# Mask by activation bias, maxima turned ahead of the max rows, and reordered seams in a four-layer cross-attention kernel

## The reference, cut to what matters

```python
# x, ctx: (8 batches, 128 tokens, 128 features); 16 heads
# L0: heads of width 8, with a mask over the keys
s = einsum('bqhd,bkhd->bhqk', q, k) / sqrt(8)
s = s * m - (1 - m) * 1e10
x = layer_norm(softmax(s) @ v @ wo + bo + x) * gamma + beta
# L1: heads of width 64, no mask, no scaling
h = x * rsqrt(mean(x**2) + 1e-6) * norm_w
x = x + softmax((h @ wq) (ctx @ wk)^T) (ctx @ wv) @ wo
# L2 block: layer norm, causal block-sparse self-attention (width 8, a small
# router picks blocks), residual; layer norm, cross-attention on ctx
# ("LC", width 8), residual; layer norm, 128 -> 512 -> 128 with relu, residual
# L3: cross-attention on ctx (width 8), residual, layer norm -> output
```

## Time and profile before

| | |
|---|---|
| median of 3 runs | 388.83 us (388.61 to 389.29) |
| profiled execution | 389.39 us, span 387.6 us |
| PE matmul busy | 333.5 us (86% of the span) |
| DVE busy | 241.7 us (62%) |
| ACT busy | 196.9 us (51%) |
| POOL busy | 96.3 us (25%) |
| mean granted clock of PE | 0.978 of full speed |
| chain that ended last, by engine | PE 63%, DVE 15%, ACT 10%, issue 8%, DMA 2% |

### The profile page before, as it was taken

The page is one execution under the profiler, slowest core; times in us unless marked ns, Lnnn a source line. Parts: engine busy times, 40 slices in busy tenths (PEclk is TensorE's granted clock), DMA queues, the critical chain, the costliest instruction groups (busy, mean ns, idle before and its releaser), DMA issues.

```text
span 387.6 us, 9184 instructions
## 1 busy us (share of the span) xinstructions
PE 333.5 (86%) x3653; PEld 215.5 (56%) x3653; DVE 241.7 (62%) x458; ACT 196.9 (51%) x419; POOL 96.3 (25%) x286
## 2 busy tenths in 40 slices
PE   5988998992899999998898998878888999899891
PEld 2424555672687778867553544355555665565450
DVE  6243475459285666758647767897657537556744
ACT  1544655644667786777413444344455453354450
POOL 7043352210000000001217223134243314323321
PEclk9999999996799999999989999999999999999998
DMA  7391000000000000000100101000100000000000
GB/s 231 125 396 44 2 3 2 2 2 0 2 0 2 3 0 2 2 2 14 42 0 2 56 15 41 17 3 22 36 33 12 2 15 11 5 16 9 22 15 27
DMA packets 7450, 11.94 MB, mean 31 GB/s; under 512 B 2024, under 2 KB 4464, under 8 KB 7152
## 3 DMA queue, kind: packets, MB, share of 16 engines
q1 hardware_dynamic: 6720, 10.04, 7.5%
q10 hardware_dynamic: 688, 1.32, 0.9%
HBM read 6.63 MB, written 0.52 MB: 18 GB/s over the span
## 4 chain that ended last, share of the span: by engine, by line
PE 63%; DVE 15%; ACT 10%; issue 8%; DMA 2%; POOL 1%; ACTq 1%; POOLq 0%
PE psum L281 16%; PE psum L337 7%; PE psum L666 5%; PE psum L290 4%; PE psum L311 4%; PE psum L717 3%; PE psum L691 3%; DVE maxs L461 3%; ACT probs L766 3%; PE psum L575 3%; PE psum L725 3%; PE psum L702 2%; PE psum L642 2%; DVE probs L471 2%; DMA xnT<-in_xt 2%
## 5 line engine op out<-in xcount | busy, mean ns | idle before, releaser
L461 DVE TENSOR_REDUCE maxs<-psum 128x8 f32<-128x1024 f32 x64 | 78.2, 1223 | 72.2 <-PE psum L266 27.8
L387 ACT ACTIVATE probs<-psum 128x1024 f32<-128x1024 f32 x64 | 65.6, 1025 | 101.0 <-PE psum L311 101.0
L281 PE MATMUL psum<-km,qT 32*128 32x512 f32 x256 | 71.5, 638 | 23.1 <-ACT xnT L566 6.5
L290 PE MATMUL psum<-qm,kT 32*128 32x512 f32 x256 | 72.1, 638 | 0.7 <-ACT probs L387 0.7
L281 PEld LDWEIGHTS psum<-km,qT 32*128 32x128 f32 x256 | 20.1, 183 | 38.1 <-issue 20.3
L533 POOL TENSOR_SCALAR rstd<-stats 128x2 f32<-128x2 f32 (+1 forms) x18 | 6.7, 372 | 126.1 <-DVE stats L497 126.1
L311 PEld LDWEIGHTS psum<-mrow,sel 32*128 32x128 bf16 x512 | 19.3, 93 | 32.0 <-issue 30.2
L766 ACT ACTIVATE probs<-psum,maxs 128x128 f32<-128x128 f32 x128 | 35.0, 396 | 2.5 <-DVE maxs L811 2.5
L337 PE MATMUL psum<-probs,vpad 128*32 128x128 f32 x1024 | 34.4, 275 | 0.5 <-DVE probs L471 0.5
L437 POOL CAST mp<-maxs 128x16 bf16<-128x16 f32 x32 | 6.8, 213 | 105.9 <-DVE maxs L461 105.9
L821 DVE TENSOR_REDUCE mres<-probs 128x8 f32<-128x1024 f32 x16 | 19.5, 1218 | 21.5 <-ACT probs L766 21.5
(11 more groups left out here) (153 smaller groups left out, 617.5 us busy)
## 6 DMA issues: line engine op xcount, KB each, us to landing
km<-kT SPq DMA_DIRECT2D x30, 64.0 KB, 1.9
wmat<-in_wmat SPq DMA_DIRECT2D x1, 1856.0 KB, 12.9
qm<-qT SPq DMA_DIRECT2D x16, 64.0 KB, 1.9
wmat<-in_wmat SPq DMA_DIRECT2D x1, 1024.0 KB, 7.5
qm<-qT SPq DMA_DIRECT2D x32, 32.0 KB, 1.8
wrow<-in_wrow SPq DMA_DIRECT2D x1, 704.0 KB, 5.4
ctxT<-in_ctxt SPq DMA_DIRECT2D x2, 256.0 KB, 4.8
xnT<-in_xt ACTq DMA_DIRECT2D x2, 256.0 KB, 5.9
```

The source lines that it names most:

```text
L281: s_mm = e.matmul(bank(j), qT[rg(j), bt(b)], km[L.slot][rg(j), :, bt(b)], start=True, stop=L in (LC, L3), skip_group_check=True)
L290: e.matmul(bank(4 + a), kT[rg(j), M.slot, bt(b)], qm[rg(j), :, bt(b)], start=True, stop=False, skip_group_check=True)
L387: e.activation(probs_of(n, half), bank(4, 2), ACT.Exp, scale=layer(n).scale)\
L461: e.tensor_reduce(maxs[:, n % 2, 8 * half:8 * half + 8], bank(2 * half, 2).rearrange("p (h k) -> p h k", k=P), AX.X, ALU.max, negate=True)\
```

## The change

Part by part:

1. **The mask on the T side.** `T_more` goes. ACT's exponential in L0 takes the mask as its bias per partition (the keys lie on the partitions there); the scaling of L0's scores moves into the copy of q and k, so that the bias needs no scaling. `S_more` stays.
2. **The turned maxima.** In a step's even half, `pe_mT` of item s-1 stood behind the max rows of item s-2; it now stands between the T main products (and the mask or causal rows of S) and those max rows. On ACT the copy `act_mrow` stands ahead of the exponential of item s-2, where it stood behind it. `pool_split` becomes four operations, two of which depend on the first alone.
3. **The beginning.** PE now makes q, k, v of the first four batches, turns `kaug`, and goes on to the first scores; k and q of the other four batches stand behind both halves of item 0's scores (odd half of step 0), their v in step 1. The 16 v1 products stand in steps 1 to 6: one in an even half, two in an odd half (before: four ahead of the first score, two in step 0, then one in each half up to step 5). The a1 transposes follow in steps 6 and 7. DVE's `masked_k` of the second half stands behind the two maxima of item 0.
4. **L0 to L1.** The first scores of L1 stand ahead of the last two q chunks in step 9, and their maxima and exponentials with them; `norm0` of batches 4, 5 and 6, 7 moves from step 9 and item 0 of L1 to items 0 and 1; `dve_z` of items 6 and 7 stands right behind the first `dve_norm1`; the first transposes of item 0 (`pe_turn1`) stand ahead of the wait for those z; the T1 transposes move from items 0 and 1 to items 1 and 2.
5. **L1 to L2.** In item 7, DVE's `z1` of item 6 stands ahead of `norm1` half 1, and L2's first scores stand at places 1 and 2 where they stood at 2 and 3.
6. **LC and L3 tables.** In steps 14 to 20 the "TC" transposes move from the even to the odd half, and LC's q projection from the odd half to the even half of the next step. L3's v projections move from steps 17 and 19 to 16 and 18. On DVE the `even` table stands ahead of `dve_past` half 0.

```diff
-        L0 = Layer("L0", 0, "0", E ** -0.5, vall, ctxT, ctxT)
+        L0 = Layer("L0", 0, "0", 1.0, vall, ctxT, ctxT)
...
-            if 2 <= _n <= 5:
-                freed(_n, 1, sem("v_out_L1"), 2 * _n + 5)
+            if 1 <= _n <= 6:
+                freed(_n, 1, sem("v_out_L1"), 3 * _n - 2)
...
             if n == 0 and half == 0:
-                e.wait_ge(L1("v_out"), 6)
+                e.wait_ge(*L0.past("v_out", 1))
+                e.wait_ge(*L0.past("k_out", 2))
...
-            if m is not None and M is L0:
-                for a in range(2):
-                    T_more(e, m, mhalf, a)
             if n is not None and L is L2:
                 for j in (2 * half, 2 * half + 1):
                     s_mm = e.matmul(bank(j), identB[:, :], causal[:, 0, :].unsqueeze(1).broadcast_to([P, 4, P]),
                                     start=False, stop=True, skip_group_check=True)
                 s_mm.then_inc(sem("S_mm"), 1)
+            if turned is not None:
+                pe_mT(e, turned)
             if m is not None:
                 e.wait_ge(sem("mT_read"), m + 1)
...
-                pe_scores(e, n, 0, n2, 1)
-                if n1 is not None:
-                    pe_mT(e, n1)
+                pe_scores(e, n, 0, n2, 1, n1)
                 even(s)
...
-            e.activation(probs_of(n, half), bank(4, 2), ACT.Exp, scale=layer(n).scale)\
+            masked = mu[:, 0, n:n + 1] if layer(n) is L0 else 0.0
+            if n == 0 and half == 0:
+                e.wait_ge(sem("mask_split"), 1)
+            e.activation(probs_of(n, half), bank(4, 2), ACT.Exp, bias=masked, scale=layer(n).scale)\
...
                 if n3 is not None:
                     act_osum(e, n3)
+                if n1 is not None:
+                    act_mrow(e, n1)
                 if n2 is not None:
                     act_exp(e, n2, 1)
-                if n1 is not None:
-                    act_mrow(e, n1)
...
             e.tensor_copy(part[0], m).then_inc(chain, 1)
-            e.wait_ge(chain, 4 * n + 1)
-            e.tensor_tensor(r[0], m, part[0], ALU.subtract).then_inc(chain, 1)
-            e.wait_ge(chain, 4 * n + 2)
-            e.tensor_copy(part[1], r[0]).then_inc(chain, 1)
-            e.wait_ge(chain, 4 * n + 3)
-            e.tensor_tensor(r[1], r[0], part[1], ALU.subtract).then_inc(chain, 1)
-            e.wait_ge(chain, 4 * n + 4)
-            e.tensor_copy(part[2], r[1]).then_inc(sem("split_done"), 1)
+            e.wait_ge(chain, 3 * n + 1)
+            e.tensor_tensor(r, m, part[0], ALU.subtract).then_inc(chain, 1)
+            e.tensor_tensor(part[1], m, part[0], ALU.subtract).then_inc(chain, 1)
+            e.wait_ge(chain, 3 * n + 3)
+            e.tensor_tensor(part[2], r, part[1], ALU.subtract).then_inc(sem("split_done"), 1)
...
                 if n is not None:
                     dve_max(e, n, 0)
+                even(s)
                 if n2 is not None and layer(n2) is L2:
                     dve_past(e, n2, 0)
-                even(s)
...
                 if b == 0:
                     pe_z(e, B - 1)
+                    pe_turn1(e, 0, 0)
+                    e.wait_ge(sem("z_read"), B)
...
             dve_norm1(e, 0, 0)
+            dve_z(e, B - 2)
+            dve_z(e, B - 1)
             for b in range(B):
                 if b + 1 < B:
                     dve_max1(e, b + 1, 0)
+                else:
+                    dve_z1(e, b - 1)
                 dve_norm1(e, b, 1)
-                if b:
+                if 0 < b < B - 1:
                     dve_z1(e, b - 1)
...
             def odd0(s):
                 if s == 0:
-                    for c in (4, 5):
-                        e.wait_ge(L1("v_out"), c - 3)
-                        pe_v1(e, c, v1_bank(c))
-                if s == 1:
+                    e.wait_ge(sem("in_ctx1"), 16)
+                    pe_proj(e, L0, "k", 4, 4, 5)
+                    e.wait_ge(sem("in_xT1"), 16)
+                    pe_proj(e, L0, "q", 4, 4, 6)
+                if 1 <= s <= 5:
                     free(e, s, 1)
-                    pe_v1(e, 7, v1_bank(7))
-                if 2 <= s <= 5:
-                    free(e, s, 1)
-                    pe_v1(e, 2 * s + 5, v1_bank(2 * s + 5))
+                    pe_v1(e, 3 * s - 2, 0)
+                    pe_v1(e, 3 * s - 1, 1)
...
                 if s == 9:
+                    pe_s1(e, 0, 0)
                     e.wait_ge(L1("c_out"), 4)
                     pe_chunk(e, 0, "q", 2)
                     pe_chunk(e, 0, "q", 3)
...
-                if (b, place) == (7, 2):
+                if (b, place) == (7, 1):
                     e.wait_ge(sem("masks"), 7)
                     pe_scores(e, B, 0, None, 0)
-                if (b, place) == (7, 3):
+                if (b, place) == (7, 2):
                     pe_scores(e, B, 1, None, 0)
...
-                if s in (17, 19):
+                if s in (16, 18):
                     free(e, s, 0)
-                    pe_v(e, L3, (s - 17) // 2, 2)
-                if 14 <= s <= 20 and s % 2 == 0:
+                    pe_v(e, L3, (s - 16) // 2, 2)
+                if 15 <= s <= 21 and s % 2:
                     free(e, s, 0)
-                    pe_turn(e, "TC", s - 14, 2, 2)
+                    e.wait_ge(sem("xnT_TC"), (s - 15) // 2 + 1)
+                    pe_proj(e, LC, "q", s - 15, 2, 2)
...
                 if 14 <= s <= 20 and s % 2 == 0:
                     free(e, s, 1)
-                    e.wait_ge(sem("xnT_TC"), (s - 14) // 2 + 1)
-                    pe_proj(e, LC, "q", s - 14, 2, 0)
+                    pe_turn(e, "TC", s - 14, 2, 0)
```

More of the change, by code:

```diff
@@ L268, in S_more, with pe_scores @@
                             start=False, stop=True, skip_group_check=True)
-        def T_more(e, n, half, a):
-            L, b, j = layer(n), n % B, 2 * half + a
-            return e.matmul(bank(4 + a), kaug[rg(j), bt(b)], ones3[rg(j), :], start=False, stop=False,
-                            skip_group_check=True)
-        def pe_scores(e, n, half, m, mhalf):
+        def pe_scores(e, n, half, m, mhalf, turned=None):
             if n is not None:
@@ L432, in pool_split @@
             m = maxs[:, w, :].rearrange("p (j i) -> p j i", i=4)
-            r = [mres[:, w, k, :].rearrange("p (j i) -> p j i", i=4) for k in range(2)]
+            r = mres[:, w, 0, :].rearrange("p (j i) -> p j i", i=4)
             e.wait_ge(sem("max_done"), 2 * n + 2)
@@ L588, in act_proj @@
             e.activation(out[:, b0 * P:(b0 + nb) * P], bank(to)[:, c0:c0 + nb * P], ACT.Identity,
-                         bias=bias if bias is not None else 0.0).then_inc(sem(f"{name}_out"), 1)
+                         bias=bias if bias is not None else 0.0,
+                         scale=E ** -0.5 if L is L0 else 1.0).then_inc(sem(f"{name}_out"), 1)
         def act_v(e, L, g, to):
@@ L636, in act_a1 @@
             e.copy(a1[:, 4 * g:4 * g + 4, :], tok(bank(to))).then_inc(sem("a_out"), 1)
-        def v1_bank(c):
-            return 4 + c % 4 if c < 4 else {4: 4, 5: 5, 6: 6, 7: 0}.get(c, 0 if c % 2 else 2)
         def pe_v1(e, c, to):
@@ L661, in pe_chunk @@
                 e.wait_ge(sem("xnT_T1"), i + 1)
-            if name == "k" and (i, c) in ((1, 2), (2, 0)):
-                e.wait_ge(sem("xnT_T1"), i + 2)
+            if name == "k" and (i, c) in ((2, 0), (2, 2)):
+                e.wait_ge(sem("xnT_T1"), 3 + c // 2)
             src = xnT if name == "q" else ctxT
@@ L785, in act_l1 @@
                 i = b // 2 + 1
+                if b == 0:
+                    act_pT1(e, 0, 0)
                 if c[0]:
@@ L1300, in even2 @@
                     act_v(e, L2, 1, 2)
-                if 14 <= s <= 20 and s % 2 == 0:
-                    act_turn(e, "TC", s - 14, 2, 2, "n2_g", "n2_b")
+                if 15 <= s <= 21 and s % 2:
+                    act_proj(e, LC, "q", s - 15, 2, 2)
                 if 22 <= s <= 28 and s % 2 == 0:
@@ L1339, in _ @@
             e.wait_ge(sem("mask_mm"), 1)
-            e.tensor_scalar(mu[:, 0, :], bank(2)[:, 0:B], -1.0, -PAD / L0.scale, ALU.add, ALU.mult).then_inc(u, 1)
+            e.tensor_scalar(mu[:, 0, :], bank(2)[:, 0:B], -1.0, -PAD, ALU.add, ALU.mult).then_inc(u, 1)
             e.wait_ge(u, 1)
```

135 lines of the change are left out of this document (57 added, 78 removed).

## The result

The changed kernel took 382.3 us (median of 4 runs, 382.08 to 386.44) beside 389.06 for the kernel before (388.61 to 391.01): ratio 0.9847, 95% interval 0.9807 to 0.9886. Timed again in another session it was 382.4 and 0.9838 (0.9815 to 0.9861). The profiled execution took 382.29, of it 380.6 span; that is 7.1 less than the 389.39 of before. The forecast was 381.6, and 382.2 on the profiled execution's own scale. Of the nine executions of the changed kernel in the two sessions, eight took 382.0 to 383.4 us at a mean granted clock of 0.989 to 0.994, and one took 386.44 at 0.975.

What follows compares the result with a forecast made beforehand. PE has by far the most work, so its standstills and lower-clock stretches count. −0.6 − 4.7 − 2.1 − 1.2 − 0.3 + 1.7 = −7.2 us, from a median of 388.83 to 381.6; range 376.0 to 386.5.

Steps and rivals of the forecast that it cites:

- The beginning: Start of the kernel: first score near 11.7, item 1's second half at 19.2, 4.0 us earlier (2.5 to 5).
- L0's steps: Step 1 +0.5; steps 2 to 5 +0.75 each, 3.0; steps 6 and 7 +0.25; steps 8 and 9 −0.4.
- on ACT mrow leaves the chain, so 0.16: Even halves: mrow no longer stands between exponential and copy on ACT, saving 0.16 us.
- Form changes: Transpose ahead of the max rows: two form changes at 0.10 each, transpose at most 0.06; exponential put off 0.26.
- Rival 2: No price for the form: the transpose slips between, 23 halves gain about 0.2 each, 377.0; chance 0.15.
- L0 to L1: Seam: k chunk 3.5 us sooner, chunk to item 2's scores −3.3, T1 back +1.2; sum −4.7 (−2 to −7).
- The charge of 0.8 for the clock: Between L0 and L1: waits of 1 to 1.5 us stay, so part of the slow stretch can stay; 0.8 charged.
- Rival 3: The seams give half: PE falls to the lower clock anyway, extra norm0 delays items 0 to 2; 384.9, chance 0.20.
- L1 to L2: Seam: z1 done first, out1 of item 7 at about 196.1 instead of 198.27; −2.1 (−0.5 to −3).
- L2, LC, L3: Later layers: L2 −1.2 by DVE's table ahead of past, LC −0.3 (−2 to +1), L3 +1.7.
- Rival 5: The split decides (slower): PE and ACT wait for POOL's split in 29 even halves; 393.2 at 0.4 each, chance 0.07.
- rival 4: The beginning costs more: products double at 1.2 GHz, the 4.0 gain shrinks to 1.5; 384.1, chance 0.08.

Runs made afterwards that it cites:

- a2: Changed kernel with T's mask rows back as products for each item's second half, the exponential's bias kept for half 0 only; 382.77 us, ratio 0.985.
- c4: Kernel before with only the turned maxima moved ahead of the max rows and mrow ahead of the exponential; 392.1 us, ratio 1.0089.
- a1: Changed kernel with the turned maxima back behind the max rows and mrow back behind the exponential; 379.38 us, ratio 0.975.
- c3: Changed kernel with turned maxima and mrow moved back, plus 8 unused transposes in PE's wait in step 10; 377.78 us, ratio 0.9706.
- b1: Kernel before with one edit: DVE's z of L0's last item directly behind item 0's first norm1; 385.42 us, ratio 0.9899.
- c1: Kernel before with DVE's z of L0's last item moved behind item 0's first norm1, plus 12 unused transposes in PE's remaining idle time; 383.56 us, ratio 0.986.
- a4: Changed kernel with LC's xnT transposes, q and v products at the places of the kernel before; 382.76 us, ratio 0.9828.
- b2: Kernel before with 36 unused transposes in PE's idle time between 91 and 96 us; 387.46 us, ratio 0.9956.

## Why the prediction was right, and which steps were off

The forecast stood 0.7 us under the measured median, and on the profiled execution's scale 0.1 under it (382.2 against 382.29). So close a hit is luck: by the table the beginning, L0's steps, L2 and LC fell short by 2.4 us together (0.5, 0.8, 0.35 and 0.7), and the two seams and L3 gave 2.2 more than forecast (1.8 and 0.4). The mechanisms named were the right ones in the main: z's place, the clock, the price of the form. (The forecast's terms for the seam from L0 to L1 add up to −4.8, not −4.7, and those of L0 to −0.65; that changes 0.15 in all.)

1. **The beginning, −4.0.** Measured −3.47. The first k rows came 0.3 later than put (12.02), item 1's second half 0.5 later.
2. **L0's steps.** The odd halves of steps 2 to 5 lost 0.64, forecast 0.65 (that of step 1 lost 0.64 too, forecast 0.5). The even ones of steps 2 to 6 lost 0.22 to 0.23, that of step 7 0.18, where the forecast had 0.10. The step that failed is "on ACT mrow leaves the chain, so 0.16". A second way, over PE's v1 product, ended 0.03 before it (the rows of the kernel before, under a2), and the delay of 0.25 from the transpose lies on that way too. Six halves at 0.12, the 0.14 of step 1 and the 0.5 of the beginning are the 1.4 by which L0 was off. My own later guess, that the longer exponential (1.11 against 1.02) was the cause, fell with a2 and c4. The other flaw: the forecast let the max rows run beside S's mask rows in the odd halves only. They do in the even ones too (a1), which hid what the transpose really cost.
3. **Form changes.** 0.26 forecast, 0.24 to 0.26 measured, 0.05 for a further transpose in the same form. The Trainium skill, TensorEngine Tiling (Array Packing), Key Properties, says that a change of mode drains the array while a change of tile does not; the trace agrees. Rival 2 is out. From step 22 on two even halves (22 and 29) lost 0.10, two (30 and 31) nothing, and six (23, 24, 26, 27, 28, 32) 0.18 to 0.27, where the forecast had seven at 0.10 and three at 0.20. The size of the whole group was still too small: about 2.6 by the forecast's terms (0.7 in L0, 1.7 from step 22 on, some 0.2 between), 3.5 by c4 in the kernel before, 4.2 in the changed kernel (by a1 1.89 in L0 and 1.64 from step 22 on, by c3, which has no slow stretch there, 0.69 between).
4. **L0 to L1.** The chunk 3.8 sooner beside L0 (forecast 3.5); from the chunk to item 2's scores 9.35 (forecast 9.4); T1's return 0.9 (forecast 1.2). The charge of 0.8 for the clock was not due: PEclk was 1.00. In the kernel before, b1 and c1 split it: 3.6 us by VectorE's order, 2.3 to 2.5 by the clock. The forecast's "without T1, and mostly at full clock" had both, but not that the clock by itself is two fifths. Its reading that the fall comes behind the stall of 5.4, and that the stall of 1.46 has none behind it, was wrong: the clock fell at 90.7, behind the 1.46 and before the 5.4 (b1). The changed kernel is rid of both waits. Rival 3 is out for the executions near 382; the one at 386.44, with its clock of 0.975, has no trace, and whether it fell in a seam is open.
5. **L1 to L2.** 2.5 against 2.1. The forecast set times at the full clock against the slow ones of the earlier trace rows, and so held two parts without telling them apart: only 0.8 is the order, and 1.7 is the clock, which some executions of the old order don't lose (c4).
6. **L2, LC, L3.** −0.85 against −1.2, +0.37 against −0.3, +1.31 against +1.7. In step 13 it was −0.80 (forecast −0.9), in step 17 −1.00 (−0.95); the worst miss is step 16, +1.06 instead of +0.3. Half of the missing 1.0 is the turned group (0.69 against some 0.2 charged); the other half is the table, worth 0.2 by a4 where the forecast had 0.8 by the split given there. Why the halves of step 16 lost so much more than charged stays open. Rival 5 (POOL's split decides) is out by its 0.3 us in one wait, rival 4 by the 3.47 of the beginning. Its mechanism exists, though: in a2's execution the clock was low from 12.4 to 15.8 us, and T(0,0) came 1.3 later.

## What to carry to other kernels

A chain shortened on one engine is worth the distance to the next chain that ends at the same copy: look for the second one before pricing it. A stall can cost its length and then slow products behind it, and work that nobody needs, put into the idle time, bought the second part back in three runs here. Look at the clock row by row: a shorter wait ahead of the long one can be where it fell. A small product in another tiling form cost two form changes here, 0.2 us, beside 0.05 for itself: put it where the array changes form anyway.

## What the runs showed of the hardware

- The granted clock after a wait of 1.4 to 1.9 us is not a matter of the kernel alone. In step 10 it fell in b1, c1 and a1 and not in the kernel before, each time after 1.44 us; at the end of L1 it fell in the kernel before (0.66 in the earlier trace rows, after 1.93) and not in c4 (after 1.92), with the same order of products there. Each of these falls cost 1.5 to 1.7 us. The Trainium skill, TensorE: Matmul & The Clock Gate, What's actually happening, has activity release the throttle; b2, c1 and c3 agree: with transposes in the gap the clock stayed at 1.00 there.
- An exponential over 128 x 1024 took 1.114 us with a bias column and 1.025 without (16 and 48 of them in the changed kernel).
- Eight products over 32 partitions for the max rows and two for the mask rows ran beside each other, 0.01 apart at their start (a1), where a transpose over 128 partitions took 0.24 to 0.26 between them.
